# The order of the FFN products on TensorE in a tile step: blocks of up and down alternate, instead of down in a row and up in a row

## The chip, the cores and the metric

One core of one Trainium2 chip runs the whole program. The metric is the device time of one execution in microseconds; the median of three runs is compared. The engines are TensorE (PE), its weight loads (PEld), VectorE (DVE), ScalarE (ACT), GpSimd (POOL) and the SyncE queue (SP).

## What is computed

A graph layer over 6250 nodes with 256 features, cut here to what the last part of the kernel does:

```python
xn = _layernorm(x, axis=-1)
output_low  = relu(segment_sum(val_low[:, None]  * (xn @ weight_low)[src],  dst))   # 106250 edges
output_high = relu(segment_sum(val_high[:, None] * (xn @ weight_high)[src], dst))
x1 = x + attention_mix(output_low, output_high, relu(xn @ weight_mlp)) + mix_layer(xn)
x2 = _layernorm(x1)
w  = x2 @ wr + br
h  = gelu(x2 @ w1 + b1)          # up:   256 -> 1024, for the selected half of the rows
y  = (h @ w2 + b2) * w           # down: 1024 -> 256
out = x1 + x2 + where(selected_by_top_k(w), y, 0)
```

## The kernel before, in words

The first third of the program (to about 880 us) sorts the edges and computes the mix layer. The rest is a loop over 49 tiles of 128 nodes, written out as 50 tile steps (`pipeline`, with `stage(i, here, before1, before2, before3)` on each engine) and an `end()`. In step i four tiles are under work at once: tile i is gathered and summed, tile i-1 gets its graph weights and attention, tile i-2 gets the FFN up product, tile i-3 the FFN down product.

The gather: POOL fetches one column of 128 source rows at a time with an indirect DMA (line 665, 852 columns) into a ring of 32 columns (`gring`). SP counts landed columns into `g_ready` and, by groups of eight, tells POOL that columns are free (`col_free`) once TensorE has used them (`sel_used`, waited for at line 562). A tile has two buckets of 64 nodes. TensorE sums a bucket with ten matmuls (more where it has more columns): a selection matrix that VectorE makes (`msel`, lines 1116 and 1122) times gathered rows, 256 wide. In the middle and at the end of a bucket it increments `sel_used`.

TensorE's order in a step (`stage`, lines 1812 to 1851) is: four transposes of tile i-1's sums (line 1817), the bias of the down product into bank 7, two transposes of x2 of tile i-2 (line 1827), four matmuls with the graph weights into bank 3 (`lh`), bucket 2i into bank 0, the down product (8 matmuls, 128x256, bank 7, `y_psum`), the up product (16 matmuls, 128x128, banks 4 and 5, one `f1_psum` for each half), bucket 2i+1 into bank 1. All these products are f32, and the trace shows each f32 matmul as two records with two weight loads; all go through the helper at line 1528.

ScalarE's order in a step (lines 1483 to 1504) is: copy bank 1 (1443, waits for the last step's second bucket), copy the transposed sums (1447), relu of `lh` (1452), copy x2's transpose (1456), copy bank 0 (1490, waits for the first bucket), two small steps of the attention (1460, 1462), nine small ones of a Newton iteration (1468 to 1473, `newton`), `scale_y` of bank 7 (1481, waits for `y_psum`), and eight gelus (1438, waits for `f1_psum` by halves). In the last step (`not here`) `scale_y` and the first four gelus stand ahead of `newton`, and the other four behind it.

The down product of tile i-3 reads `fh`, which the gelus of the step before wrote. The gelus of this step overwrite `fh`; ScalarE issues them behind `scale_y`, and `scale_y` waits for the whole down product.

Of the kernel before, what the change touches and what calls it, by code (L numbers as in the profile page):

```python
# [22 lines left out]
P = 128  # L23
# [20 lines left out]
def wait(eng, sem, value):  # L44

    if isinstance(value, int) and value <= 0:
        return
    eng.wait_ge(sem, value)

def build(nc, a, out):
# [6 lines left out]
    KD = D // P  # L58
    KF = HID // P
# [39 lines left out]
    with ExitStack() as ctx:  # L99
        sems = {}  # L100

        def S(name):
            if name not in sems:
                sems[name] = ctx.enter_context(nc.semaphore(name))
            return sems[name]
# [98 lines left out]
        w1f = r2.take([P, KD, HID])  # L204
# [9 lines left out]
        x2t = r2.take([P, KD, P])  # L214
# [93 lines left out]
        part = free[:, 2 * D:3 * D].bitcast(BF16)  # L308
# [55 lines left out]
        bank = [ctx.enter_context(nc.psum_tensor(f"bank{i}", [P, 512], F32)) for i in range(8)]  # L364
# [1161 lines left out]
        def _(pe):  # L1526
            def mm(out_, lhsT, rhs, start, stop, **kw):
                return pe.matmul(out_, lhsT, rhs, start=start, stop=stop, **kw)  # L1528
# [17 lines left out]
            for g in range(G):  # L1546
                if g % (G // 2) == 0:
                    pe.wait_ge(S("digits_ready"), (H1 + H2) * (1 + g // (G // 2)))
                for u in range(BB // HG):
                    c = g * (BB // HG) + u  # L1550
                    ins = mm(bank[2 + g // PER][0:M, (g % PER) * W:(g % PER + 1) * W], oh1[:, c * M:(c + 1) * M], oh2[:, c * W:(c + 1) * W],
                             u == 0, u == BB // HG - 1)
# [3 lines left out]
            for k in range(H2):  # L1556
                ins = mm(bank[6][0:NR, 0:G], spread[0:M, k, :, :].rearrange("p h k -> p (h k)"), hcnt[0:M, :, k], k == 0, k == H2 - 1)
# [198 lines left out]
            for k in range(NBLK):  # L1756
# [6 lines left out]
                for f in range(4):  # L1763
                    ins = pe.transpose(bank[k][:, f * P:f * P + n], by_field[:, f, :], ident[0:n, 0:n])
# [10 lines left out]
            def bucket(b, acc):  # L1775

                word = bucket_word(pe, b)
                lo = first_col(pe, word)
                more = extra_cols(pe, word)
                pe.wait_ge(S("g_ready"), pe.snap(lo + VIS))  # L1780
                pe.wait_ge(S("sel_ready"), 2 * b + 1)
                for j in range(VIS):
                    ins = add_col(acc, msel[:, 2 * b % NBUF, j, :], lo + j, j == 0, False)
                ins.then_inc(S("sel_used"), 1)
                with pe.If(more > 0):
                    done = extras_so_far(pe, b)
                    with pe.Fori(0, more) as e:
                        pe.wait_ge(S("g_ready"), pe.snap(lo + e + VIS + 1))
                        pe.wait_ge(S("sel_x_ready"), pe.snap(done + e + 1))
                        add_col(acc, msel_x[:, :], lo + e + VIS, False, False).then_inc(S("sel_x_used"), 1)  # L1790
                rest = pe.snap(lo + more)
                pe.wait_ge(S("g_ready"), pe.snap(rest + BOTH))
                pe.wait_ge(S("sel_ready"), 2 * b + 2)
                for j in range(VIS):
                    ins = add_col(acc, msel[:, (2 * b + 1) % NBUF, j, :], rest + VIS + j, False, j == VIS - 1)
                ins.then_inc(S("sel_used"), 1)

            def up(part):

                for f in range(part * KF // 2, (part + 1) * KF // 2):  # L1800
                    for k in range(KD):
                        ins = mm(bank[4 + part][:, (f % 4) * P:(f % 4 + 1) * P], w1f[:, k, f * P:(f + 1) * P], x2t[:, k, :],
                                 k == 0, k == KD - 1)
                return ins

            def down(lo, hi):

                for f in range(lo, hi):
                    ins = mm(bank[7][:, 0:D], fh[:, f, :], w2f[:, f, :], False, f == KF - 1)
                return ins  # L1810

            def stage(i, here, before1, before2, before3):
                if before1:
                    pe.wait_ge(S("agg_b"), i)
                    for k in range(KD):
                        for h in range(2):
                            ins = pe.transpose(bank[2][:, k * D + h * P:k * D + (h + 1) * P], agg[:, h, k * P:(k + 1) * P], ident[:, :])  # L1817
                    ins.then_inc(S("at_psum"), 1)
                if before3:

                    wait(pe, S("y_ready"), i - 3)
                    mm(bank[7][:, 0:D], ones_b[0:65, :], b2f3[0:65, :], True, False)
                    pe.wait_ge(S("fh_ready"), (i - 2) * KF)
                if before2:
                    pe.wait_ge(S("x2_ready"), i - 1)
                    for k in range(KD):
                        ins = pe.transpose(bank[6][:, k * P:(k + 1) * P], x2n[:, k * P:(k + 1) * P], ident[:, :])
                    ins.then_inc(S("xt_psum"), 1)
                if before1:
                    if isinstance(i, int) and i == 1:  # L1830
                        pe.wait_ge(S("gnn_loaded"), 16 * 2)
                    pe.wait_ge(S("aggt_ready"), i)
                    wait(pe, S("lh_ready"), i - 1)
                    for v, w in enumerate((wlow, whigh)):
                        for k in range(KD):
                            ins = mm(bank[3][:, v * D:(v + 1) * D], aggt[:, k, v, :], w[:, k, :], k == 0, k == KD - 1)
                    ins.then_inc(S("lh_psum"), 1)
                if here:
                    wait(pe, S("agg_a"), i)
                    bucket(2 * i, bank[0])  # L1840
                if before3:
                    down(0, KF).then_inc(S("y_psum"), 1)
                if before2:
                    if isinstance(i, int) and i == 2:
                        pe.wait_ge(S("ffn_loaded"), 16 * 2)
                    pe.wait_ge(S("x2t_ready"), i - 1)
                    for part in range(2):
                        up(part).then_inc(S("f1_psum"), 1)
                if here:
                    wait(pe, S("agg_b"), i)  # L1850
                    bucket(2 * i + 1, bank[1])
# [3 lines left out]
            def count_total(r):  # L1855
                pe.wait_ge(S("cnt_ready"), r + 1)
                mm(bank[0][:, 0:15], ones_f[:, :], cnt[:, :], True, True).then_inc(S("cnt_total"), 1)

            def down_bias(a):
                wait(pe, S("y_ready"), a)  # L1860
                mm(bank[7][:, 0:D], ones_b[0:65, :], b2f3[0:65, :], True, False)

            def end():

                down_bias(T - 2)
                pe.wait_ge(S("x2_ready"), T)
                for k in range(KD):
                    ins = pe.transpose(bank[6][:, k * P:(k + 1) * P], x2n[:, k * P:(k + 1) * P], ident[:, :])
                ins.then_inc(S("xt_psum"), 1)
                pe.wait_ge(S("fh_ready"), (T - 1) * KF)  # L1870
                down(0, KF).then_inc(S("y_psum"), 1)
                count_total(0)
                pe.wait_ge(S("x2t_ready"), T)
                up(0).then_inc(S("f1_psum"), 1)
                count_total(1)
                up(1).then_inc(S("f1_psum"), 1)
                count_total(2)
                down_bias(T - 1)
                pe.wait_ge(S("fh_ready"), T * KF)
                down(0, KF // 2)  # L1880
                count_total(3)
                down(KF // 2, KF).then_inc(S("y_psum"), 1)
                for r in range(4, 8):
                    count_total(r)

            pipeline(pe, stage, end)
            pe.wait_ge(S("eq_ready"), 1)
            mm(bank[0][:, 64:64 + T], before[:, :], eqb[:, :], True, True)
# [27 lines left out]
```

## Time and profile before

| | |
|---|---|
| median of 3 runs | 2526.34 us (2504.72 to 2528.77) |
| profiled execution, span from first to last instruction | 2481.7 us |
| that span below the lowest and the median run | 23.0 us, 44.6 us |
| mean granted TensorE clock | 0.835 |
| TensorE matmuls busy | 1719.4 us (69%), 9109 records |
| VectorE, ScalarE, GpSimd busy | 50%, 37%, 55% |
| chain that ended last | PE 51%, "issue" 23%, DVE 10%, ACT 9% |

How to read it: for the profiled execution the span alone is given, and it does not say which of the three times is its own; every term of a sum is taken from the span and added to the median. A start of a matmul is recorded, its end is modelled; what tells its true end is when an engine that waits for it starts. "issue" is idle time for which the profile shows no releaser, "remote" a wait whose releaser the profile could not place. Two stretches matter: 945 to 2367 us holds 45 full tile steps, 2367 to 2416 the last two.

### The profile page before, as it was taken

Reading aid. Unit: us, or ns where it says so; the run is one execution under the profiler, and the core shown is the slowest. Engines: PE = TensorE matmul, PEld = TensorE weight load, DVE = VectorE, ACT = ScalarE, POOL = GpSimd, SP = SyncE. Lnnn points to the kernel's source line nnn. Section 1 sums busy time; section 2 is a strip of 40 time slices with the busy share of each in tenths; the row PEclk is TensorE's granted clock in tenths of the full one; section 3 lists DMA queues with packets and bytes.
Section 4 is the critical chain, followed back from the end, with each engine's and each line's share of the span. In section 5 each row is a group of like instructions: output and inputs, shape, how many; then the busy total and the mean of one; then the engine's idle time right before and its main releaser. Section 6 shows DMA issues by size and latency. Waiting matters only on the chain.

```text
span 2481.7 us, 30518 instructions
## 1 busy us (share of the span) xinstructions
PE 1719.4 (69%) x9109; PEld 1441.9 (58%) x9109; DVE 1229.1 (50%) x3164; ACT 924.8 (37%) x2641; POOL 1371.7 (55%) x1351
## 2 busy tenths in 40 slices
PE   4788884998865347776777677677577677667672
PEld 4566673887754335665665666566466566556562
DVE  8899995888761223432343333333333333333336
ACT  2677873777652112321222222222222222222223
POOL 3277675788776565545555455455455545554600
PEclk9899996999967667888887888788788788788886
DMA  3221211111100422222222222222222222222303
GB/s 90 72 63 54 80 33 30 46 54 46 46 5 5 133 85 72 78 69 75 71 74 71 68 73 75 65 72 75 68 73 75 75 69 71 81 71 68 85 9 104
DMA packets 102212, 162.99 MB, mean 66 GB/s; under 512 B 32190, under 2 KB 72762, under 8 KB 102040
## 3 DMA queue, kind: packets, MB, share of 16 engines
q0 software_dynamic: 55232, 113.59, 16.4%
q1 hardware_dynamic: 46808, 47.29, 6.0%
q8 instruction: 85, 1.39, 0.2%
q14 instruction: 87, 0.71, 0.1%
HBM read 139.76 MB, written 21.04 MB: 65 GB/s over the span
## 4 chain that ended last, share of the span: by engine, by line
PE 51%; issue 23%; DVE 10%; ACT 9%; another core or an unknown queue 5%; DMA 1%; SPq 1%; POOL 0%; DVEq 0%; ACTq 0%; POOLq 0%
PE bank L1528 49%; ACT side L1303 2%; PE bank L1817 1%; ACT base L1303 1%; ACT arena L1303 1%; DVE arena L811 1%; ACT arena L1447 1%; ACT arena L1443 1%; DVE arena L733 1%; ACT side L1519 1%; DVE arena L766 1%; ACT arena L1307 0%; PE bank L1602 0%; DVE arena L781 0%
## 5 line engine op out<-in xcount | busy, mean ns | idle before, releaser
L1528 PE MATMUL bank<-arena 128*128 128x128 f32 (+3 forms) x6320 | 1292.5, 359 | 508.2 <-issue 426.8
L1528 PEld LDWEIGHTS bank<-arena 128*128 128x128 f32 (+1 forms) x6320 | 1094.8, 205 | 683.8 <-issue 500.0
L665 POOL DMA_INDIRECT arena<-xn_rows,arena x852 | 825.5, 969 | 733.8 <-SPq L564 450.0
L648 POOL DMA_INDIRECT sorted_records<-arena x448 | 523.0, 1167 | 256.0 <-issue 139.3
L1167 DVE CUSTOM_DVE_ANT_0 arena<-arena 128x256 f32<-128x256 f32 x98 | 37.8, 423 | 414.9 <-ACT arena L1452 376.1
L1122 DVE TENSOR_TENSOR arena<-arena 128x640 f32<-128x640 bf16 (+1 forms) x204 | 164.2, 805 | 47.6 <-DVE arena L1116 17.7
L1172 DVE SCALAR_TENSOR_TENSOR att_prod<-sg,att_neg 128x9 f32<-128x9 f32 x49 | 8.5, 174 | 334.9 <-issue 300.8
L1490 ACT ACTIVATE arena<-bank 128x256 f32<-128x256 f32 x49 | 18.8, 383 | 355.5 <-remote 262.1
L1116 DVE SCALAR_TENSOR_TENSOR arena<-io,arena 128x320 bf16<-128x320 f32 (+1 forms) x204 | 97.8, 479 | 106.3 <-DVE wall L1209 43.5
L1528 PE MATMUL bank<-arena,base 128*128 128x128 f32 (+3 forms) x766 | 118.4, 287 | 16.7 <-ACT base L1307 8.3
L1438 ACT ACTIVATE arena<-bank,b1f 128x128 f32<-128x128 f32 x392 | 110.3, 372 | 33.5 <-PE bank L1528 28.1
L811 DVE TENSOR_TENSOR arena<-arena 128x1280 f32<-128x1280 bf16 x84 | 120.5, 1488 | 4.1 <-remote 1.7
L1528 PEld LDWEIGHTS bank<-arena,base 128*128 128x128 f32 (+2 forms) x766 | 110.2, 211 | 17.6 <-ACT base L1307 8.5
L1443 ACT ACTIVATE arena<-bank 128x256 f32<-128x256 f32 x49 | 18.8, 383 | 247.0 <-PE bank L1528 219.3
L1528 PE MATMUL bank<-side,arena 128*128 128x512 f32 x196 | 97.1, 619 | 0.3 <-issue 0.3
L1481 ACT ACTIVATE side<-bank,wall 128x256 f32<-128x256 f32 x49 | 23.1, 472 | 176.0 <-remote 165.3
L1303 ACT ACTIVATE base<-arena 128x128 f32<-128x128 f32 x280 | 84.7, 391 | 9.4 <-DVE arena L792 9.4
L1468 ACT ACTIVATE nr<-nri 128x1 f32<-128x1 f32 x49 | 9.9, 203 | 206.0 <-issue 159.8
L1303 ACT ACTIVATE arena<-arena 128x128 f32<-128x128 f32 x280 | 84.6, 397 | 0.0
L1303 ACT ACTIVATE side<-arena 128x128 f32<-128x128 f32 x280 | 84.6, 392 | 0.0
L1528 PE MATMUL bank<-arena,side 128*128 128x128 f32 x560 | 73.5, 282 | 12.0 <-issue 10.9
L1528 PEld LDWEIGHTS bank<-arena,side 128*128 128x128 f32 x560 | 68.0, 196 | 15.6 <-issue 14.1
(312 smaller groups left out, 1889.2 us busy)
## 6 DMA issues: line engine op xcount, KB each, us to landing
arena<-xn_rows,arena POOLq DMA_INDIRECT x852
sorted_records<-arena POOLq DMA_INDIRECT x448
arena<-in_x SPq DMA_DIRECT2D x12, 512.0 KB
xn_rows<-arena SPq DMA_DIRECT2D x12, 512.0 KB
x_plus_xn_rows<-arena SPq DMA_DIRECT2D x12, 512.0 KB
arena<-x_plus_xn_rows SPq DMA_DIRECT2D x12, 512.0 KB
arena<-xn_rows SPq DMA_DIRECT2D x12, 512.0 KB
out<-base SPq DMA_DIRECT2D x4, 1024.0 KB
```

The lines of the kernel that those rows point to most:

```text
L648: pool.indirect_dma_start(rec_dram, bass.IndirectOffsetOnAxis(ap=idx[0:PR, par, u:u + 1], axis=0), stage_rec[0:PR, par, u * 8:(u + 1) * 8] ...
L665: pool.indirect_dma_start(gring[:, c % GR, :], None, xn_dram, bass.IndirectOffsetOnAxis(ap=rring[:, c, 3:4].bitcast(I32), axis=0)).then_in ...
L733: ins = dve.tensor_tensor(oh[:, t, :].rearrange("p j (h e) -> p j h e", e=2), twice[:, t, :].unsqueeze(2).to_broadcast([P, GS, NB // 2, 2] ...
L766: dve.tensor_tensor(prod4[:, :, :, 0:NB], oh[:, :, :].rearrange("p (s j) b -> p s j b", s=GROUPS), rankf[:, :].rearrange("p (s b) -> p s b ...
L811: dve.tensor_tensor(cellrec[:, t, :].rearrange("p t (f c) -> p t f c", f=4), cell[:, t, :].unsqueeze(2).to_broadcast([P, GS, 4, GC]), raw[ ...
L1116: return dve.scalar_tensor_tensor(out_, io64[:, :].unsqueeze(1).to_broadcast([P, n, BK]), float(BK * b), r[:, :, 0:1].to_broadcast([P, n, ...
L1122: return dve.tensor_tensor(out_, hots.unsqueeze(2).to_broadcast([P, n, 2, BK]), r[:, :, 1:3].unsqueeze(3).to_broadcast([P, n, 2, BK]), ALU ...
L1167: ins = dve.tensor_tensor_reduce(out=lg_prod[:, k, :], in0=lh[:, k * D:(k + 1) * D], in1=att_rows[:, k, :], scale=1.0, scalar=0.0, op0=ALU ...
L1303: ins = act.activation(quot[:, j, :], iota32[:, :], ACT.Abs, bias=p32[:, par, s * GS + j:s * GS + j + 1], scale=-1.0)
L1438: act.activation(fh[:, f, :], bank[4 + part][:, (f % 4) * P:(f % 4 + 1) * P], ACT.Gelu_apprx_tanh, bias=b1f[:, f:f + 1]).then_inc(S("fh_re ...
L1443: act.activation(agg[:, 1, :], bank[1][:, 0:D], ACT.Copy).then_inc(S("agg_b"), 1)
L1528: return pe.matmul(out_, lhsT, rhs, start=start, stop=stop, **kw)
```

## The change

The 8 matmuls of the down product and the 16 of the up product are the same before and after. Before, all of down comes first and then all of up; now, for each f of 0 to 7, the two up matmuls of block f are followed by the down matmul of block f. The wait for `x2t_ready` stands ahead of all 24, and `y_psum` is incremented by the last of the 24. `end()` keeps its order.

```diff
+            def up_block(f):
+
+                for k in range(KD):
+                    ins = mm(bank[4 + f // 4][:, (f % 4) * P:(f % 4 + 1) * P], w1f[:, k, f * P:(f + 1) * P], x2t[:, k, :],
+                             k == 0, k == KD - 1)
+                if f % 4 == 3:
+                    ins.then_inc(S("f1_psum"), 1)
...
                 if here:
                     wait(pe, S("agg_a"), i)
                     bucket(2 * i, bank[0])
-                if before3:
-                    down(0, KF).then_inc(S("y_psum"), 1)
                 if before2:
...
                     pe.wait_ge(S("x2t_ready"), i - 1)
-                    for part in range(2):
-                        up(part).then_inc(S("f1_psum"), 1)
+                for f in range(KF):
+                    if before2:
+                        up_block(f)
+                    if before3:
+                        ins = down(f, f + 1)
+                if before3:
+                    ins.then_inc(S("y_psum"), 1)
                 if here:
                     wait(pe, S("agg_b"), i)
                     bucket(2 * i + 1, bank[1])
```

TensorE in a full step, from the last matmul of the first bucket (bank 0) to the head of the second bucket (L406), before; bank 7 is down, banks 4 and 5 are up:

```order
L1528 MATMUL bank0<-arena 128x256
L1528 MATMUL bank7<-arena 128x256 x8
L1528 MATMUL bank4<-arena 128x128 [waits x2t_ready]
L1528 MATMUL bank4<-arena 128x128 x7
L1528 MATMUL bank5<-arena 128x128 x8
L406 TENSOR_LOAD packed [waits agg_b]
```

The same place now, its beginning and then its end:

```order
L1528 MATMUL bank0<-arena 128x256
L1528 MATMUL bank4<-arena 128x128 [waits x2t_ready]
L1528 MATMUL bank4<-arena 128x128
L1528 MATMUL bank7<-arena 128x256
L1528 MATMUL bank4<-arena 128x128 x2
```

```order
L1528 MATMUL bank7<-arena 128x256
L1528 MATMUL bank5<-arena 128x128 x2
L1528 MATMUL bank7<-arena 128x256
L1528 MATMUL bank5<-arena 128x128 x2
L1528 MATMUL bank7<-arena 128x256
L406 TENSOR_LOAD packed [waits agg_b]
```

The block of 24 now ends with two short matmuls and a long one, where it ended with sixteen short ones; no instruction is added or removed.

TensorE in the last step (i = 49, no buckets), from the graph weights (bank 3) to the bias of the next down product, before and then now:

```order
L1528 MATMUL bank3<-arena 128x256 x3
L1528 MATMUL bank7<-arena 128x256 x8
L1528 MATMUL bank4<-arena 128x128 [waits x2t_ready]
L1528 MATMUL bank4<-arena 128x128 x7
L1528 MATMUL bank5<-arena 128x128 x8
L1528 MATMUL bank7<-b2f3,ones_b 128x256 [waits y_ready]
```

```order
L1528 MATMUL bank7<-arena 128x256
L1528 MATMUL bank5<-arena 128x128 x2
L1528 MATMUL bank7<-arena 128x256
L1528 MATMUL bank7<-b2f3,ones_b 128x256 [waits y_ready]
```

The last down matmul stands right ahead of the bias that waits for `y_ready`, and sixteen up matmuls stood between them. The order on VectorE, ScalarE and SP is unchanged.

## Rows read from the trace of the kernel before

**Rows 1.** Groups of instructions by form, TensorE, 945 to 2367 us

```profile
line engine op names shapes xcount | busy us, mean ns | idle before us <-releasers
...
L1528 PE MATMUL bank<-arena 128*128 128x128 f32 x1440 | 275.3, 326 | 370.5 <-issue 367.2 <-DVE arena L1122 2.5
L1528 PE MATMUL bank<-arena 128*128 128x256 f32 x1080 | 252.5, 383 | 18.7 <-ACT arena L1447 17.9 <-issue 0.8
```

**Rows 2.** Waits, 900 to 2400 us: us in total, times, longest

```profile
POOL arena L665 <- SPq L564: 443.6, 66, 13.1
PE bank L1528 <- issue: 386.4, 285, 9.2
ACT side L1481 <- remote: 165.3, 42, 11.4
```

**Rows 3.** Timeline, TensorE, the step from 1505: start, us, what, count [idle before]

```profile
1506.40 11.77 PE L1528 MATMUL bank<-arena 128*128 128x256 f32 x62 [0.42 <-issue]
...
1518.75 0.27 PE L1528 MATMUL bank<-arena 128*128 128x128 f32 x1 [0.58 <-issue]
...
1525.77 0.37 PE L1528 MATMUL bank<-arena 128*128 128x128 f32 x1 [1.73 <-issue]
1527.18 7.54 PE L1528 MATMUL bank<-arena 128*128 128x128 f32 x30 [1.04 <-issue]
```

**Rows 4.** Windows of that step: PE, PEld, DVE, ACT, POOL busy, clock, DMA share, GB/s

```profile
1512.55:1516.00 3.45, 3.45 (x17) 3.04 (x16) 0.53 (x4) 0.77 (x3) 2.54 (x4) 1.00 0.39 114
1516.00:1518.02 2.02, 2.02 (x19) 1.98 (x17) 1.81 (x9) 0.00 (x0) 1.72 (x2) 1.00 0.42 108
1518.02:1527.18 9.16, 1.46 (x6) 1.24 (x5) 5.43 (x17) 2.65 (x9) 5.25 (x6) 0.66 0.31 91
1527.18:1529.28 2.10, 2.10 (x10) 2.07 (x10) 1.09 (x3) 1.50 (x5) 0.00 (x0) 0.50 0.00 0
1529.28:1531.20 1.92, 1.92 (x7) 1.56 (x6) 1.73 (x4) 1.14 (x4) 0.00 (x0) 0.50 0.03 9
1531.20:1534.50 3.30, 3.30 (x17) 2.75 (x15) 0.00 (x0) 0.00 (x0) 0.95 (x1) 1.00 0.00 0
```

**Rows 5.** Timeline, GpSimd, the same step: the last gather and the next

```profile
1523.81 0.99 POOL L665 DMA_INDIRECT arena<-xn_rows,arena  x1 [0.30 <-issue]
1533.53 0.95 POOL L665 DMA_INDIRECT arena<-xn_rows,arena  x1 [8.74 <-SPq L564]
```

**Rows 6.** Timeline, ScalarE, the same step, and one row of VectorE

```profile
1508.93 0.38 ACT L1456 ACTIVATE arena<-bank 128x256 f32<-128x256 f32 x1
1514.53 0.38 ACT L1490 ACTIVATE arena<-bank 128x256 f32<-128x256 f32 x1 [5.22 <-remote]
...
1522.78 0.29 ACT L1473 ACTIVATE nr<-nr 128x1 f32<-128x1 f32 x1
1527.36 0.47 ACT L1481 ACTIVATE side<-bank,wall 128x256 f32<-128x256 f32 x1 [4.29 <-remote]
...
1534.76 0.38 ACT L1443 ACTIVATE arena<-bank 128x256 f32<-128x256 f32 x1 [4.08 <-PE bank L1528]
...
1522.83 0.82 DVE L1122 TENSOR_TENSOR arena<-arena 128x640 f32<-128x640 bf16 x1
```

**Rows 7.** Timeline, TensorE, the first row after the stall in four other steps

```profile
1407.86 7.25 PE L1528 MATMUL bank<-arena 128*128 128x128 f32 x28 [1.73 <-issue]
...
1950.12 7.80 PE L1528 MATMUL bank<-arena 128*128 128x128 f32 x31 [1.04 <-issue]
...
2173.72 5.85 PE L1528 MATMUL bank<-arena 128*128 x20 [0.36 <-issue]
...
1025.85 6.27 PE L1528 MATMUL bank<-arena 128*128 x20 [4.71 <-DVE arena L1122]
```

**Rows 8.** Timeline, ScalarE and then TensorE, the last step

```profile
2414.18 1.14 ACT L1438 ACTIVATE arena<-bank,b1f 128x128 f32<-128x128 f32 x4 [1.31 <-PE bank L1528]
2415.68 0.20 ACT L1468 ACTIVATE nr<-nri 128x1 f32<-128x1 f32 x1 [0.36 <-DVE nri L1197]
...
2415.77 0.27 PE L1528 MATMUL bank<-b2f,ones_b 65*128 65x256 bf16 x1
```

More of the change, by code:

```diff
@@ L1796, in bucket @@
                 ins.then_inc(S("sel_used"), 1)
+            def up_block(f):
[4 more added lines that the diff above has]
+                    ins.then_inc(S("f1_psum"), 1)
             def up(part):
                 for f in range(part * KF // 2, (part + 1) * KF // 2):
[L1801 to L1804, printed above, removed]
+                    up_block(f)
             def down(lo, hi):
@@ L1846, in stage @@
                     pe.wait_ge(S("x2t_ready"), i - 1)
-                    for part in range(2):
-                        up(part).then_inc(S("f1_psum"), 1)
+                for f in range(KF):
+                    if before2:
+                        up_block(f)
+                    if before3:
+                        ins = down(f, f + 1)
+                if before3:
+                    ins.then_inc(S("y_psum"), 1)
                 if here:
@@ L1873, in end @@
                 pe.wait_ge(S("x2t_ready"), T)
-                up(0).then_inc(S("f1_psum"), 1)
+                up(0)
                 count_total(1)
-                up(1).then_inc(S("f1_psum"), 1)
+                up(1)
                 count_total(2)
```

## The prediction

> **What bounds the kernel now.** I read the waits first. GpSimd waits 443.6 us for SP to free ring columns, and TensorE's largest wait is 386.4 us of "issue" [rows 2]. The groups by form put that idle time almost wholly ahead of the 128x128 matmuls, the up product: 367.2 us in 45 steps (1440 records, 32 in a step), and nearly nothing ahead of the 256-wide ones [rows 1]. So something stops TensorE in the middle of up, in nearly every step.
>
> The timeline of one step shows where. From 1506.40 come 62 records without a break: 8 of the graph weights, 20 of the first bucket, 16 of down, 18 of up. Then four records come one by one until 1525.77, and from 1527.18 thirty more: the last 10 of up and the 20 of the second bucket [rows 3]. The windows give the speeds. Down goes at 3.45 / 16 = 0.216 us a record, up at 2.02 / 18 = 0.112, both at clock 1.00 (2.4 GHz); in the stall the clock falls to 0.50 (1.2 GHz), the 10 records after it take 0.21 each, and the full clock is back at 1531.20, in the middle of the second bucket [rows 4].
>
> What releases TensorE is the end of the gather, not a producer of its data. The last gather is issued at 1523.81 and none is under way after about 1526; the DMA share is 0.31 in the stall and 0.00 from 1527.18 [rows 4, 5]. ScalarE shows the same from outside: `scale_y` needs only the down product, whose last record starts before 1516.0, and ScalarE is free from 1523.07, yet it starts at 1527.36, just after the release; it waits so for 165.3 us in all [rows 2, 6]. Even bank 0's copy, which needs the first bucket (its last record starts near 1512.3), starts at 1514.53 [rows 6]. I read it thus: while gathers run back to back, TensorE's completions come out late, only so many matmuls can be open at once, and when that number is reached it issues no faster than they drain. When the gathers end all drains at once. The cause inside the chip no row shows.
>
> The loop that sets the pace then is: first half of the second bucket done, columns freed, about 16 gathers at 1.25 us (0.95 and 0.30 [rows 5]), drain, release, rest of up, first half of the second bucket. GpSimd idles 8.74 us in it [rows 5]. Whatever TensorE still owes at the release stands on the path one for one. Elsewhere in the step its order is free.
>
> **The change part by part.** No instruction is added or taken away, so the work of the block is the same: 16 x 0.216 + 32 x 0.112 = 7.0 us. Three things move.
>
> First, what is left at the release. If the stall comes at the same count of records, as many stay behind: 62 before the stall, four slow, ten left here; eight in the step whose row after the stall has x28, eleven in one with x31 [rows 3, 7]. I read all 45 steps so: 41 have such a tail, mostly 8 to 10 records; in four nothing is left (two of them are the x20 rows [rows 7]). Before, the tail is all up. Now the last ten records of the block are up 2, down 2, up 4, down 2: four of them are down. Each costs 0.216 - 0.112 = 0.104 us more at full clock and 0.21 more at half clock. The low clock after the release lasts until 1531.20, whatever stands in the row, and the first half of the second bucket ends after that (its 10 records begin at 1529.28, and 5 are done by then). Four records at half clock put 0.83 us of bucket work from the slow part into the fast one, and half of it comes back: 4 x 0.104 = 0.42 us later. With the lesser tails, 41 steps give about 17 us. The bounds are 41 x 0.83 = 34 us, if none comes back, and below.
>
> Below nothing: if the stall comes at the same time and not at the same count, 5.47 us after the block's start (1512.55 to 1518.02) [rows 4], then (at 0.147 us a record, the block's mean) 37 records are out instead of 34, 11 remain, five go slowly, and the last six are four up and two down: 0.88 us at full clock against ten up, 1.12. That is -0.24 a step, -10 us in all. I take the count: the steps whose rows after the stall have x28, x30 and x31 stop within three records of one another [rows 3, 7], and from the last record whose completion ScalarE saw (the 28th of the 62, at 1514.53 [rows 6]) to the stall there are 34 open.
>
> Second, `y_psum` comes with the last record of the block. ScalarE then has `scale_y` (0.47 [rows 6]) and eight gelus (2 x 1.14 [rows 8]) to do before it copies bank 1, 2.75 us in all; the second bucket's 20 records take 4.3 us even at full clock, so the copy at 1534.76, on the path, stays where it is relative to the bucket. That cover leaves 1.5 us. Before, the first gelus ran beside the tail; now they run beside the bucket. Third, the wait for `x2t_ready` is moved up by 3.45 us. Its copy ended at 1509.31 [rows 6], the block begins at 1512.55: 3.2 us of cover, nothing queued behind it is held. VectorE's selection for the second bucket ends at 1523.65 [rows 6], 5.6 us ahead of its use, so it stays hidden too. Where no tail is left VectorE is what is late (4.71 us) [rows 7], and those steps stay as they are.
>
> At the end there is one exposed place. In the last step ScalarE runs `scale_y` and four gelus ahead of `newton`. Before, the gelus wait for up at 2414.18 and `newton` starts at 2415.68 on its own input [rows 8]. Now y is complete when the block ends, near 2415.9 (the bias behind it starts at 2415.77 now [rows 8]); scale 0.47, gelus 1.14, `newton` at about 2417.5: 1.8 us later, and the last tile's x2 and all behind it with it. Taken at 2 us.
>
> The sum is 17 + 2 = 19 us on the span of 2481.7, which makes 2501. The median of the runs lies 44.6 us above the span and the fastest run 23.0; I add the 19 to the median: 2545.
>
> **The rivals.** One: the whole price at half clock. If the clock comes back later because the block is, or if the first half of the bucket ends before it does, the four long records cost 0.83 us: 34 + 2 = 36 us, 2562, slower by 1.4%. The place is between release and the first half of the second bucket, and it decides once that half lies wholly in the 0.50 stretch. For it: here only 5 of its 10 records are past the boundary; the return of the clock falls differently in each step. Against: in nearly all 45 the half ends after the return.
>
> Two: time-bound stall, -10 + 2 = -8 us, 2518. For it: the stall starts about 13.0 us into most steps. Against: the counts above, which before could not come apart from time.
>
> Three: the order makes the stall end earlier or not leave a tail, as in the x20 rows. After the release a step then needs about 6.3 us (2173.72 to the next step at 2180.04) against 8.0 in the step of rows 3 (1527.18 to 1535.19). At 1.5 us in 41 steps that is 62 us, 2466, faster by 2.4%. For it: such steps exist. Against: in them the gathers had paused, and the new order does not touch GpSimd.
>
> Four: no effect in the tail, since long and short records change places with no net work: 2 us, 2528.
>
> **How the numbers follow.** The forecast has 0.47, rival one 0.17, two 0.16, three 0.08, four 0.12. About 1% (25 us) is what a measurement of this kernel can tell from no change; its own three runs span 24. Slower by over 1% is rival one and the upper end of the forecast, where gathers and steps fall less well together: 0.26. Faster by over 1% is rival three and a little of two: 0.10. The rest, 0.64, is within 1%. The range goes from 2512 (rival two with some luck) to 2568 (rival one with some bad).
>
> **What would show it.** In the profile after: the x62-like row ahead of the stall stays at 62 records, but ends 0.5 us earlier (34 records at 0.147 are 5.0 us instead of 5.5); idle time by form is split between 128x128 and 128x256; the rows after the stall keep about 30 records and last some 0.4 us longer; `scale_y` starts at the end of the block, not at the release; bank 1's copy follows the bucket at once. I am wrong if the stall takes 65 or more records before it starts (rival two), if steps of 26 us become common (three), or if the copy of bank 1 (L1443) waits for gelus.

## The result, and the profile after

The changed kernel took 2530.68 us (median of 19 runs, 2500.47 to 2590.41); the kernel before, beside it, 2506.54 us (19 runs, 2476.39 to 2581.89). The ratio is 1.0077, 95% interval 1.0047 to 1.0106: slower by some 0.8%, which is 19 us of 2506.54; the two medians lie 24 us apart. The ratio is taken from the shorter runs of each kernel alone (eleven of each, within 1.5% of its fastest), and the profiled execution below is one of the longer ones. The forecast was 19 us of slowdown on a base of 2526.34, so 2545; the base of this comparison is 20 us lower, which is more than all that was to be measured.

The profiled execution of the changed kernel has a span of 2588.7 us, 107 longer than that of before. Most of this is no effect of the change: its first tile step begins at 969.3 us where it began at 889.9, and nothing ahead of it was edited. So I compare steps and not spans. The same 45 full steps take 1421.8 us before (945 to 2367 us) and 1446.1 us now (1025 to 2471 us), 24 us more. The waits in these two stretches, before and then now (us in total, times, longest):

```profile
POOL arena L665 <- SPq L564: 426.6, 64, 13.1
PE bank L1528 <- issue: 368.8, 280, 3.2
```

```profile
POOL arena L665 <- SPq L564: 451.6, 62, 13.7
PE bank L1528 <- issue: 383.8, 301, 4.6
ACT side L1481 <- PE bank L1528: 271.3, 41, 16.5
```

GpSimd's wait for free columns has grown by 25 us, as much as the steps have. TensorE's stall has grown by 15 us; it begins earlier now and ends when it did (see the section on the prediction). `scale_y` (L1481) waits longer, 271.3 against 165.3 [rows 2], and by name for TensorE now: y comes with the block's end. The groups by form, TensorE, the same stretch now, answer to [rows 1]:

```profile
L1528 PE MATMUL bank<-arena 128*128 128x256 f32 x1080 | 359.8, 429 | 146.4 <-issue 126.2 <-ACT arena L1447 17.0 <-DVE arena L1122 2.5
L1528 PE MATMUL bank<-arena 128*128 128x128 f32 x1440 | 284.2, 307 | 251.2 <-issue 250.6
```

The idle time that stood ahead of the short matmuls alone is now split, 250.6 and 126.2: the stall falls on whichever kind is next. TensorE's timeline of a step with a tail of ten records, as in [rows 3]:

```profile
1862.60 11.15 PE L1528 MATMUL bank<-arena 128*128 128x256 f32 x62 [0.42 <-ACT arena L1447]
1874.60 0.38 PE L1528 MATMUL bank<-arena 128*128 128x256 f32 x1 [0.85 <-issue]
...
1881.70 0.37 PE L1528 MATMUL bank<-arena 128*128 128x128 f32 x1 [1.76 <-issue]
1884.50 7.54 PE L1528 MATMUL bank<-arena 128*128 128x128 f32 x30 [2.42 <-issue]
1892.51 0.66 PE L1822 MATMUL bank<-ident,arena 128*128 128x128 f32 x4 [0.47 <-ACT arena L1443]
```

Again 62 records, four singles and 30, but the 62 take 11.15 us and not 11.77. ScalarE in this step, as in [rows 6]:

```profile
1887.70 0.47 ACT L1481 ACTIVATE side<-bank,wall 128x256 f32<-128x256 f32 x1 [8.88 <-PE bank L1528]
1888.07 2.17 ACT L1438 ACTIVATE arena<-bank,b1f 128x128 f32<-128x128 f32 x8
1892.08 0.38 ACT L1443 ACTIVATE arena<-bank 128x256 f32<-128x256 f32 x1 [1.84 <-PE bank L1528]
```

`scale_y` starts 3.2 us after the release (1884.50), the gelus run beside the second bucket, and the copy of bank 1 still waits 1.84 us for TensorE, not for the gelus.

The step shown here and that of [rows 3] show no difference from the release to the next step: 8.01 us in both. The clock came back 4.0 us after the release in the one and 3.2 in the other, and such scatter covers 0.4 us. It takes all steps. From each step's timeline I took three numbers: the records of the block left at the release (taken as the last record that starts 0.6 us or more after the one before it), the time from the release to the next step's first transpose, and the number of records of the step up to the stall (7 of them transposes and bias). The means over the steps with a tail:

```
kernel                    steps  short  long  to next step, us (+-standard error)
before                       41    8.6   0     8.08 +-0.09
changed                      40    5.0   3.8   8.50 +-0.10
up, then down                40    0     7.6   8.75 +-0.11
y_psum late only             41    8.0   0     7.97 +-0.08
alternating, ups last        41    7.8   0     8.05 +-0.08
down, up, up                 41    5.9   2.0   8.15 +-0.08
```

The difference of the first two rows is 0.42 us. It hangs a little on where the stall is said to end: with 0.5 us in place of 0.6 it is 0.31, and from the last idle gap of 0.2 us or more it is 0.51. The length of a whole step needs no such choice. In the 40 pairs of steps that have a tail in both kernels it rose by 0.43 +-0.12 us, 17 us in all. The other five pairs add 7 us, 4.9 of it in one step of the changed kernel (from 1557.1 us): there the stall began after 59 records, and the second bucket then waited for VectorE. Whether the change did that or chance, one step does not show.

### The profile page after: what moved, and what is told of

It is laid out like the page before. It is cut to its first block, busy times and chain, and to the rows that moved or that the text cites. A ratio compares the mean times of both kernels' runs of the same rounds, so it can differ in the third digit from the quotient of the medians.

```text
span 2588.7 us, 30518 instructions
## 1 busy us (share of the span) xinstructions
PE 1789.0 (69%) x9109; PEld 1470.8 (57%) x9109; DVE 1228.9 (47%) x3164; ACT 920.4 (36%) x2641; POOL 1348.7 (52%) x1351
## 4 chain that ended last, share of the span: by engine, by line
PE 59%; issue 23%; DVE 7%; ACT 6%; another core or an unknown queue 4%; DMA 0%; SPq 0%; DVEq 0%; ACTq 0%; POOL 0%; POOLq 0%
PE bank L1528 57%; PE bank L1822 1%; PE bank L1602 1%; ACT base L1303 1%; ACT side L1303 1%; ACT arena L1443 1%; ACT arena L1447 1%; ACT side L1519 1%; ACT arena L1303 0%; DVE arena L811 0%; DVE arena L733 0%; DMA arena<-sorted_records 0%; DVE arena L1122 0%; DVE arena L1116 0%
## 5 line engine op out<-in xcount | busy, mean ns | idle before, releaser
L1528 PE MATMUL bank<-arena 128*128 128x256 f32 (+3 forms) x6320 | 1338.6, 365 | 509.4 <-issue 442.7
L1528 PEld LDWEIGHTS bank<-arena 128*128 128x128 f32 (+1 forms) x6320 | 1110.5, 208 | 720.9 <-issue 547.4
L648 POOL DMA_INDIRECT sorted_records<-arena x448 | 501.7, 1120 | 356.2 <-DVE arena L829 161.3
L1490 ACT ACTIVATE arena<-bank 128x256 f32<-128x256 f32 x49 | 18.8, 384 | 364.1 <-remote 220.8
L1481 ACT ACTIVATE side<-bank,wall 128x256 f32<-128x256 f32 x49 | 23.2, 473 | 295.9 <-PE bank L1528 287.2
L1528 PE MATMUL bank<-arena,side 128*128 128x128 f32 x560 | 85.8, 292 | 49.9 <-issue 48.6
L1528 PEld LDWEIGHTS bank<-arena,side 128*128 128x128 f32 x560 | 75.1, 204 | 55.0 <-issue 53.5
L1528 PE MATMUL bank<-side,arena 128*128 128x512 f32 x196 | 102.7, 649 | 0.0
L766 DVE TENSOR_TENSOR arena<-arena 128x2940 f16<-128x2940 bf16 x28 | 47.3, 1690 | 113.7 <-ACT arena L1313 57.9
L1326 ACT ACTIVATE arena<-bank 128x512 f32<-128x512 f32 (+1 forms) x50 | 29.2, 585 | 198.4 <-remote 157.8
```

Of the source, the lines that this page charges most:

```text
L648: pool.indirect_dma_start(rec_dram, bass.IndirectOffsetOnAxis(ap=idx[0:PR, par, u:u + 1], axis=0), stage_rec[0:PR, par, u * 8:(u + 1) * 8] ...
L766: dve.tensor_tensor(prod4[:, :, :, 0:NB], oh[:, :, :].rearrange("p (s j) b -> p s j b", s=GROUPS), rankf[:, :].rearrange("p (s b) -> p s b ...
L1326: act.activation(xt[:, pr, :, 0:n, :], psT[:, :, 0:n, :], ACT.Copy).then_inc(S(ready), 1)
```

## The experiments

The theory to be tested: what the block still owes at the release is on the path, so only the kinds of its last records matter. The first four runs change the order alone. They shared one chip, with a median before of 2467.88.

**Up, then down.** The two rows of the block change places, so that the tail is all long.

```diff
-                if before3:
-                    down(0, KF).then_inc(S("y_psum"), 1)
                 if before2:
...
                         up(part).then_inc(S("f1_psum"), 1)
+                if before3:
+                    down(0, KF).then_inc(S("y_psum"), 1)
```

> All 16 up matmuls in a row, then all 8 of down in a row; y_psum comes with the last of the block, as in the changed kernel. Tail theory (what is left of the block at the release decides): the 8 to 10 records left in 41 steps are all down, so each costs 0.104 us more than before at full clock: 9 x 0.104 x 41 = 38 us and 2 for the last step, ratio to before 1.016 (1.012 to 1.025). Late-y theory (ScalarE gets y_psum late and its gelus hold the next step): the same lateness as in the changed kernel, so the same ratio, 1.008. Alternation theory (changing between banks 7 and 4/5 costs TensorE time): only one change, so about 1.000 to 1.001.

Measured: 2495.36, ratio 1.0103 (1.0062 to 1.0144). The direction is right and it is the slowest of the four, but below the expected size: the stall comes 0.7 to 0.8 us earlier than in the changed kernel, more records come out one by one in it, and 7.6 are left, not the 8.6 that I had counted with. 8.75 - 8.08 = 0.67 us in 40 steps is 27 us, 1.1%. The interval also holds the 1.008 of the late y; the next run decides that.

**`y_psum` late, order as before.** Only the signal moves, to the last block of up.

```diff
-                    down(0, KF).then_inc(S("y_psum"), 1)
+                    down(0, KF)
...
+                            if before3 and f == KF - 1 and k == 0:
+                                ins.then_inc(S("y_psum"), 1)
```

> TensorE's order is that of before (down in a row, then up in a row); only the increment of y_psum is moved from the last down matmul to the 15th of the 16 up matmuls, so ScalarE's scale_y and gelus start as late as in the changed kernel. Tail theory: the tail is all up, 1.000 in the tile steps and 2 us in the last step, ratio 1.001 (0.997 to 1.005). Late-y theory: 1.008. Alternation theory: 1.000.

Measured: 2471.0, ratio 1.0024 (0.9996 to 1.0051). The late y is not what costs 0.8%: the upper end, 1.0051, lies below the change's 1.0077, though not below its interval, and the steps show no rise at all (7.97 us against 8.08).

**Alternating, with ups last.** Down and up alternate one by one, and eight ups (16 short records) close the block.

```diff
+            ORDER = [('d', 0), ('u', 0), ('d', 1), ('u', 1), ('d', 2), ('u', 2), ('d', 3), ('u', 3), ('d', 4), ('u', 4), ('d', 5), ('u', 5), ('d', 6), ('u', 6), ('d', 7), ('u', 7), ('u', 8), ('u', 9), ('u', 10), ('u', 11), ('u', 12), ('u', 13), ('u', 14), ('u', 15)]
```

> One down and one up matmul alternate eight times, then the last eight up matmuls stand in a row: more changes of bank than in the changed kernel, but the last 16 records are all up, so the tail at the release is as before. y_psum comes with the 15th of the 24. Tail theory: 1.000 (0.996 to 1.004). Alternation theory: as much as the changed kernel or more, 1.008 to 1.012. Late-y theory: 1.001 to 1.003, since y is less late.

Measured: 2469.73, ratio 0.9994 (0.9965 to 1.0024). Alternation has no price of its own.

**Down, up, up.** As the change, but each down stands ahead of its two ups, which leaves one down (two records) in the last ten.

```diff
+            ORDER = [('d', 0), ('u', 0), ('u', 1), ('d', 1), ('u', 2), ('u', 3), ('d', 2), ('u', 4), ('u', 5), ('d', 3), ('u', 6), ('u', 7), ('d', 4), ('u', 8), ('u', 9), ('d', 5), ('u', 10), ('u', 11), ('d', 6), ('u', 12), ('u', 13), ('d', 7), ('u', 14), ('u', 15)]
```

> The changed kernel's alternation with the down matmul ahead of the two up matmuls of each round instead of behind them. Of the last 10 records 2 are down (4 in the changed kernel). Tail theory: 2 x 0.104 x 41 = 9 us and 1 to 2 us at the end, ratio 1.004 (1.000 to 1.008). Alternation theory: 1.008. Late-y theory: y comes 0.45 us earlier than in the changed kernel, so 1.006 to 1.008.

Measured: 2476.12, ratio 1.0038 (1.0019 to 1.0057), as the tail theory had it: half the price of the change for half of its long records in the tail. The interval overlaps that of the late `y_psum` (1.0024) and that of the change (1.0077), so the times alone do not show the halving.

The next four ask for the stall itself, beside a median before of 2470.59.

**No gathers.** GpSimd leaves out every gather after the first 32 columns, and SP counts the columns left out in place of landed ones; the rest works on the old rows.

```diff
+                if c >= GR:
+                    pool.sem_inc(S("skipped"), 1)
+                    continue
                 pool.indirect_dma_start(
```

> Leaves out the gather of all columns but the first 32: GpSimd only counts a column as landed, so the sums use stale rows, and TensorE, VectorE and ScalarE do the same instructions as before. Gather theory (back-to-back gathers hold up TensorE's completions and so stop it in up): no issue stall in the up product; scale_y starts within 1 us of the end of down; a step is then limited by the chain over VectorE and TensorE, 20 to 26 us against 31, the whole 2150 to 2350 us. Rival, instruction supply (the stall belongs to a place in TensorE's own stream): the stall stays where it is, after some 62 records, about 8 us a step.

Measured: 1983.32 us, one run, below the expected range: I had underrated the whole stall with all that hangs on it. TensorE's timeline of a step:

```profile
1512.52 13.34 PE L1534 MATMUL bank<-arena 128*128 128x256 f32 x76 [0.42 <-ACT arena L1453]
1526.86 4.58 PE L1534 MATMUL bank<-arena 128*128 x20 [1.00 <-DVE arena L1128]
1531.91 0.66 PE L1823 MATMUL bank<-ident,arena 128*128 128x128 f32 x4 [0.47 <-ACT arena L1449]
```

All 76 records of weights, first bucket, down and up run without a break; 1.00 us of waiting for VectorE is what is left of the stall, a step takes 20.8 us, and the clock stays at 1.00 in it. The completions are no longer late either. ScalarE's copy of bank 0, which needs the first 28 of these records:

```profile
1518.87 0.38 ACT L1496 ACTIVATE arena<-bank 128x256 f32<-128x256 f32 x1 [3.44 <-PE bank L1534]
```

It starts 6.35 us after the first record (1512.52), where it started 8.13 us after it before (1506.40 and 1514.53 [rows 3, 6]).

**Narrow gathers.** The same number of gathers, but each row is 64 bytes instead of 1024 (other data; `xn_fine` is the same table seen as rows of 16 values).

```diff
-                    gring[:, c % GR, :], None, xn_dram,
+                    gring[:, c % GR, 0:D if c < GR else 16], None, xn_dram if c < GR else xn_fine,
```

> The same 852 gathers with the same number of descriptors, but 16 values a row (64 bytes) instead of 256, read from another place of the same table, so the sums are of other data. It tells the number of descriptors and GpSimd's issue from the bytes moved. If bytes cause the stall: no stall, a step of 24 to 28 us. If descriptors or GpSimd's issue cause it: the stall stays in up, and a step changes by less than 1 us (the last transfer lands a little earlier).

Measured: 2472.72 us, one run, as before. The window of its stall shows why this tells much (PE, PEld, DVE, ACT, POOL busy, clock, DMA share, GB/s):

```profile
1516.80:1525.60 8.80, 1.19 (x5) 0.86 (x4) 5.83 (x14) 2.65 (x9) 4.77 (x5) 0.67 0.06 6
```

The DMA moves 6 GB/s at a share of 0.06, against 91 and 0.31 [rows 4], and the stall is as long. Bytes are not its cause; that gathers are issued and run at all is. GpSimd's issuing and the DMA's own work on each row were not told apart.

**VectorE's second selection ahead of the attention.** Only VectorE's stage is edited.

```diff
                     bucket(2 * i)
+                    bucket(2 * i + 1)
                 if before1:
                     post_a(i - 1)
-                if here:
-                    bucket(2 * i + 1)
```

> VectorE makes the selections of the second bucket right behind those of the first, ahead of the attention's steps, instead of behind them; TensorE's order is that of before. Theory: in the 41 steps with a tail these selections were ready some 5 us before their use, so nothing changes there; only the four steps without a tail gain up to 4 us each. Ratio 0.993 to 1.002. Rival (the second bucket's start hangs on VectorE and not on the release): 0.95 or less.

Measured: 2463.37, ratio 0.996 (0.9932 to 0.9987). A step with 16 gathers in it:

```profile
1378.89 12.89 PE L1527 MATMUL bank<-arena 128*128 128x256 f32 x72 [0.42 <-ACT arena L1446]
...
1400.21 7.22 PE L1527 MATMUL bank<-arena 128*128 x20 [1.07 <-issue]
```

72 records where most steps with 16 gathers had 62 to 66, four singles, and at the release only the 20 of the bucket: the tail is gone in fifteen such steps. In nearly all others 4 to 10 records of it stay. The ratio lies where I expected it, but I had expected no change in the steps with a tail. The fifteen steps are also a test of the theory, and it comes out in part: a tail of some 7.5 short records should be worth 7.5 x 0.112 = 0.8 us, and the steps take 30.25 us in the mean against 30.78 in the run with narrow gathers, which has TensorE's and VectorE's orders of before: 0.5 us less. Why not the whole, no run shows.

**Both buckets in a row.** The second bucket moves ahead of down and up on TensorE (with VectorE's order as in the run above).

```diff
                     bucket(2 * i, bank[0])
+                    wait(pe, S("agg_b"), i)
+                    bucket(2 * i + 1, bank[1])
                 if before3:
...
-                if here:
-                    wait(pe, S("agg_b"), i)
-                    bucket(2 * i + 1, bank[1])
```

> As the last one, and TensorE sums the second bucket right behind the first, ahead of down and up. Theory (what TensorE still owes ahead of the second bucket at the release stands on the loop release, tail, half a bucket, free columns, gathers): the bucket is now issued before the stall, so the columns are free at the release, and the next gathers start 4 to 5 us earlier; rest of up runs beside them. 41 steps at 3 to 5 us: 120 to 200 us less, ratio 0.92 to 0.95. Rival (the loop hangs on something else, such as ScalarE or the transposes): 0.98 or more.

Measured: 2663.53, ratio 1.0788 (1.0742 to 1.0835). A miss with the wrong sign. Timelines of ScalarE, TensorE and GpSimd, then the group of the transposes from 970 to 2400 us:

```profile
1536.61 2.18 ACT L1437 ACTIVATE arena<-bank,b1f 128x128 f32<-128x128 f32 x8 [1.78 <-PE bank L1527]
1538.63 0.43 ACT L1442 ACTIVATE arena<-bank 128x256 f32<-128x256 f32 x1
```

```profile
1505.52 1.12 PE L1816 MATMUL bank<-ident,arena 128*128 128x128 f32 x4 [2.30 <-ACT arena L1442]
...
1507.38 18.30 PE L1527 MATMUL bank<-arena 128*128 128x256 f32 x90
```

```profile
1513.81 0.94 POOL L665 DMA_INDIRECT arena<-xn_rows,arena  x1 [13.62 <-SPq L564]
```

```profile
L1816 PE MATMUL bank<-ident,arena 128*128 128x128 f32 x161 | 45.1, 435 | 383.2 <-ACT arena L1442 383.2
```

The stall now catches the end of up. After the release come the last up, eight gelus (2.18), the copy of bank 1, the transposes, the weights and only then the buckets that free the columns; GpSimd idles 13.62 us. The rival that I had named, a loop that hangs on ScalarE or the transposes, is what the order brought about: the transposes wait 383.2 us in all for the copy of bank 1, which stands behind the gelus. I had looked at what stands ahead of the second bucket in its step and not at what stands between the release and the next bucket: the second bucket right behind the release had been in the good place.

The last three follow from that: keep the bucket at the release and take the tail away from ahead of it. Median before: 2499.19.

**Half of up behind the second bucket.**

```diff
-                    for part in range(2):
-                        up(part).then_inc(S("f1_psum"), 1)
+                    up(0).then_inc(S("f1_psum"), 1)
                 if here:
                     wait(pe, S("agg_b"), i)
                     bucket(2 * i + 1, bank[1])
+                if before2:
+                    up(1).then_inc(S("f1_psum"), 1)
```

> The order of the kernel before, but the second half of up (8 matmuls, 16 records) stands behind the second bucket. Tail theory (what stands between the release and the first half of the second bucket is on the path one for one): the 8 to 9 records of up that stood there, 1.7 us in 40 steps, are gone from the path, since 67 records stand ahead of the bucket and the stall begins at 61 to 70; the work behind the bucket lies under the next gathers. Full gain 68 us or 2.7%; in the run with VectorE's order changed, steps without a tail were only 0.4 to 0.8 us shorter, which gives 16 to 32 us. I expect a ratio of 0.975 to 0.993, and in the trace a bucket that follows the release at once. Rival (the block as such bounds the step, wherever it stands): 1.000. A second rival: the gelus of the second half now hold up ScalarE's copy of bank 1, and the next step starts later; that delay is hidden under the stall by the tail theory and is 1.5 us a step, 1.03, if it is not.

Measured: 2352.79, ratio 0.9432 (0.9382 to 0.9481). The sign is right and the size is twice what the whole tail was worth. Its waits, 900 to 2250 us, then a step on TensorE, GpSimd, VectorE and ScalarE:

```profile
POOL arena L665 <- SPq L564: 279.1, 86, 9.2
...
PE bank L1528 <- issue: 139.8, 56, 7.6
```

```profile
1524.29 0.66 PE L1817 MATMUL bank<-ident,arena 128*128 128x128 f32 x4 [1.50 <-ACT arena L1443]
...
1525.69 13.23 PE L1528 MATMUL bank<-arena 128*128 128x256 f32 x60 [0.42 <-ACT arena L1447]
1541.91 6.36 PE L1528 MATMUL bank<-arena 128*128 x36 [2.99 <-issue]
1549.78 0.66 PE L1817 MATMUL bank<-ident,arena 128*128 128x128 f32 x4 [1.50 <-ACT arena L1443]
```

```profile
1534.66 0.94 POOL L665 DMA_INDIRECT arena<-xn_rows,arena  x1 [3.01 <-SPq L564]
...
1547.13 0.94 POOL L665 DMA_INDIRECT arena<-xn_rows,arena  x1 [2.09 <-SPq L564]
```

```profile
1540.78 0.83 DVE L1122 TENSOR_TENSOR arena<-arena 128x640 f32<-128x640 bf16 x1
```

```profile
1542.10 0.29 ACT L1473 ACTIVATE nr<-nr 128x1 f32<-128x1 f32 x1
1542.30 0.46 ACT L1481 ACTIVATE side<-bank,wall 128x256 f32<-128x256 f32 x1
```

This step takes 25.5 us (1524.29 to 1549.78); most take 27, and the mean of 45 full steps is 28.2 where it was 31.6. TensorE's largest wait by "issue" is 139.8 us, not 386.4, with 83.4 more that the profile puts down to VectorE, and in such a step it is another kind of wait: all 60 records ahead of the bucket are out, and the bucket starts 0.30 us after VectorE's selection (1540.78 + 0.83). That holds in 44 of the 45 steps (0.30 to 0.34 us), so what sets the bucket's start here is VectorE and no longer the release. GpSimd issues 8 gathers, pauses 3.01 us, issues 8, and pauses again, where it had one pause of 8.74 and some 16 in a row; and `scale_y` no longer waits for a completion, it follows `newton` at once. So it is not only the tail that went: the stall itself is gone from most steps. That the split rows of gathers let the completions out is my reading; no run tests it, and how much of the 5.7% is the tail I did not separate. The second rival did come true in part: the transposes wait 1.50 us for the bank 1 copy behind the gelus, where they waited 0.47.

**The same, with down and the first half of up alternating.** One matmul of up, one of down, eight times, stands ahead of the second bucket.

```diff
-                    down(0, KF).then_inc(S("y_psum"), 1)
...
+                for n in range(KF):
+                    if before2:
+                        f, k = divmod(n, KD)
+                        ins = mm(bank[4][:, f * P:(f + 1) * P], w1f[:, k, f * P:(f + 1) * P], x2t[:, k, :],
+                                 k == 0, k == KD - 1)
...
+                    if before3:
+                        ins = down(n, n + 1)
```

> As the run with half of up behind the second bucket, but the 8 matmuls of up that stay ahead of it alternate with the 8 of down (one up, one down). Tail theory: nothing or nearly nothing is left of the block at the release, so the order inside it costs nothing; the same time as that run within 0.3%. Rival (alternation has a price of its own, at any place): 0.8% slower than that run, as the change was against the kernel before.

Measured: 2349.53, ratio 0.9403 (0.934 to 0.9466), no slower than the run above. The alternation that cost 0.8% ahead of the second bucket costs nothing where it isn't in the tail. Here too the bucket starts 0.30 to 0.33 us after VectorE's selection, in all 45 steps.

**Half of up behind the second bucket, with VectorE's second selection early.** Both edits shown above together: `up(1)` behind the bucket, and `bucket(2 * i + 1)` ahead of `post_a(i - 1)`.

> As the run with half of up behind the second bucket, and VectorE selects for the second bucket before it does the attention of the tile before. If in that run VectorE's selection has become what is late at the release in some steps (the row of the second bucket with a wait for VectorE, 4.7 us before in a step without a tail), this takes it away: 0 to 1% faster than that run. If nothing was late there: the same within 0.3%.

Measured: 2358.08, ratio 0.9449 (0.9393 to 0.9505), the same as without, which is the second of the two outcomes that I had written down. But its reason, that nothing was late, does not hold: the selection was what the bucket waited for. Two steps of this run on TensorE:

```profile
1582.59 14.75 PE L1527 MATMUL bank<-arena 128*128 128x256 f32 x67 [0.42 <-ACT arena L1446]
...
1602.62 0.59 PE L1527 MATMUL bank<-arena 128*128 x1 [2.36 <-issue]
1603.38 5.89 PE L1527 MATMUL bank<-arena 128*128 x26 [0.17 <-issue]
...
1612.18 16.65 PE L1527 MATMUL bank<-arena 128*128 128x256 f32 x87 [0.42 <-ACT arena L1446]
```

The selection is now ready 9 us or more ahead of the bucket, and the stall is back in about half of the steps, mostly inside the second bucket (23 steps of 33.0 us in the mean), while the others run nearly without a break (22 steps of 23.0 us). The mean of 28.1 us is near that of the two runs above, by another way. So the equal times do not say that VectorE's order is idle here; it trades one wait for another, and why they come out even no run shows.

## Why the prediction was right, step by step

**The tail, 17 us.** Right in mechanism and size. Four long records were to be in it; 3.8 were. The cost was to be 0.42 us a step, in 41 steps; from the release to the next step the mean rose by 8.50 - 8.08 = 0.42 us (the standard errors leave +-0.13), in 40 steps: 17 us, and whole steps give the same. That it comes out to the hundredth is luck. That this is the kinds in the tail, and neither alternation nor the late y, the runs with order changes show: all-short tails lie at 0.9994 and 1.0024, two long records at 1.0038, nearly eight at 1.0103.

**Half price, not whole (rival one).** The clock returned 4.35 us after the release in the mean, in both kernels. The first half of the second bucket was signalled 5.45 us after it before and 5.88 after, so it ends behind the return, and half of the slow part's cost comes back as I had argued. The whole price would have been 3.8 x 0.21 = 0.8 us a step, and up-then-down, with 7.6 long records, would have cost 1.6 and not 0.67.

**Count or time (rival two).** Not settled as I had put it. In steps with 16 gathers the stall came after 70.6 records of the step before and 70.6 after, 0.5 us earlier, as forecast. In those with 14 it came after 68.4 and then 64.5, 1.3 us earlier: neither the same count nor the same time. So the step of the prediction that fixed the tail, the same count of records ahead of the stall, did not hold in the steps with 14 gathers. The tail kept its 8 to 9 records all the same, since more came out one by one in the longer stall; that the two made up for each other was luck. Nor could my sign for rival two, 65 records or more in the row ahead of the stall, have told: four steps with a tail now have 65, and before two had 65 and 66. The Trainium skill ("TensorE: Matmul & The Clock Gate", Architectural detail) gives TensorE a queue of 64 instructions. No row shows the queue: with 62 records ahead of one stall and 72 ahead of another (with VectorE's selection early), a fixed count from the step's start is out, and whether a fixed number of open ones fits is not shown. Time-boundness would have made the change faster, and it isn't.

**The release.** It stayed where the gathers put it: 21.18 us after the step's start with 14 gathers and 23.27 with 16, to the hundredth the same in both kernels. Rival three (the stall ends earlier) is out; no effect at all (rival four, 2 us) is out by the interval.

**The hidden parts.** The late y and the gelus stayed hidden, with 1.84 us to spare in the step shown, where I had 1.5, and 1.78 or more in every step with a tail. VectorE's selection stayed hidden in these steps too; the step at 1557.1 us is the exception named above.

**The last step, 2 us.** The term was undersized. VectorE, ScalarE and TensorE there:

```profile
2519.26 0.15 DVE L1197 TENSOR_SCALAR nri<-nri 128x1 int32<-128x1 int32 x1
```

```profile
2522.35 0.23 ACT L1468 ACTIVATE nr<-nri 128x1 f32<-128x1 f32 x1
```

```profile
2513.64 7.29 PE L1528 MATMUL bank<-arena 128*128 128x128 f32 x48 [0.96 <-ACT arena L1456]
```

`newton` starts 2.9 us after its input is there, where it started at once [rows 8]. 0.96 of this is the wait for `x2t_ready`: I had priced that wait at nothing because a bucket covers it, and in the last step there is no bucket. Down used to fill that place. The other 2.0 us is near the 1.8 that I had worked out without it.

**The base.** 2526.34 was the median of three runs; 19 runs gave 2506.54. The forecast lies 14 us above the 2530.68 measured, and its base alone lies 20 us too high; with the right base it would have been 2526, 5 us too low. The rise was to be 19 us, and 19 us by the ratio or 24 by the medians were measured.

## What to carry to other kernels

When an engine is stopped by its own late completions, find the event that releases it and list what it still has to do from there to the next thing that others wait for: only that list is on the path. Reordering ahead of the stop cost nothing that could be told (0.9994 and 1.0024), and long work in the list costs its difference. Moving work behind the awaited item can be worth far more than the list itself (5.7% here), but then another wait sets the pace, and the list has to be made anew: two runs of equal time can wait for quite different things. Check a hidden wait again in the first and last steps, where its cover may not be there.

## What the runs showed of the hardware that I had not expected

TensorE's completions are held up by GpSimd's row gathers as such: without them the kernel takes 1983 us and not 2471, and with a sixteenth of the bytes (6 GB/s against 91 in the stall) it takes 2473. The end of the gathers goes with the release of TensorE in every order that kept the second bucket's place and VectorE's order: the release comes 2.3 to 2.6 us (median of each run) after GpSimd's last gather, with wide rows and with narrow ones. Which part of the chip the two share no run showed.
